# Quantised attention: one of two heads' scores read in one pass of 2048, the other in two of 1024

## The reference

```python
q = _fq_sym(q, axis=-1)      # 8 bit steps, one scale per row
k = _fq_sym(k, axis=-1)
v = _fq_sym(v, axis=2)
attn = jnp.einsum('bhqd,bhkd->bhqk', q, k)
attn = jax.nn.softmax(attn.astype(jnp.float32), axis=-1)
attn = _fq_unsigned(attn, axis=-1)     # round(x / (max/255)), 0..255
out = jnp.einsum('bhqk,bhkd->bhqd', attn, v)
return out @ Wp + bp
```

## Time and profile before

| what | us |
|---|---|
| median of 3 runs (2371.12 to 2379.82) | 2379.8 |
| the profiled execution, its own time | 2377.23 |
| its span | 2375.4 |
| busy in the span: PE / DVE / ACT / POOL | 2047.6 / 1697.0 / 1339.2 / 873.4 |
| busy share of the span: PE / DVE / ACT / POOL | 86% / 71% / 56% / 37% |
| the loop of the change, first to last instruction | 1384.4 to 2028.5 |

### The profile page before, as it was taken

The page is one execution under the profiler, slowest core; times in us unless marked ns, Lnnn a source line. Parts: engine busy times, 40 slices in busy tenths (PEclk is TensorE's granted clock), DMA queues, the critical chain, the costliest instruction groups (busy, mean ns, idle before and its releaser), DMA issues. The chain is left out here.

```text
span 2375.4 us, 49288 instructions
## 1 busy us (share of the span) xinstructions
PE 2047.6 (86%) x17593; PEld 1100.0 (46%) x17617; DVE 1697.0 (71%) x3048; ACT 1339.2 (56%) x1808; POOL 873.4 (37%) x730
## 2 busy tenths in 40 slices
PE   3776999999997785899996789999999999558855
PEld 1343555556564564488863423333333333434533
DVE  4775755555555557843356899999999999567975
ACT  3454633333335675633332568888888888445565
POOL 4750000000002561500053347777777777224301
PEclk8887999999997897999996755555555555788989
DMA  6343222222224007222322036666666665010110
GB/s 206 89 173 120 71 65 68 62 71 66 66 66 142 24 2 268 84 50 68 64 80 98 1 58 107 108 107 107 107 108 107 108 108 108 13 71 2 20 21 27
DMA packets 384870, 195.32 MB, mean 82 GB/s; under 512 B 312301, under 2 KB 355311, under 8 KB 382703
## 3 DMA queue, kind: packets, MB, share of 16 engines
q1 hardware_dynamic: 381617, 184.47, 32.5%
q0 software_dynamic: 3072, 8.39, 1.1%
HBM read 94.99 MB, written 23.09 MB: 50 GB/s over the span
## 5 line engine op out<-in xcount | busy, mean ns | idle before, releaser
L2429 POOL CAST qa_pT<-qa_eT 128x2048 bf16<-128x2048 uint8 x256 | 483.4, 1893 | 162.1 <-DMA qa_eT<-qa_e 120.8
L2442 PE MATMUL qa_S<-qa_kT,qa_qT 32*128 32x512 f16 x1024 | 514.4, 616 | 4.8 <-DVE qa_scores L2494 3.4
L2478 ACT ACTIVATE qa_e<-qa_scores,qa_nb 128x2048 uint8<-128x2048 f32 x256 | 510.4, 1994 | 4.4
L2494 DVE TENSOR_SCALAR_CACHE_REDUCE qa_scores<-qa_S,qa_sq,qa_mx 128x1024 f32<-128x1024 f32 x256 | 335.8, 1358 | 0.0
L2494 DVE TENSOR_SCALAR_CACHE_REDUCE qa_scores<-qa_S,qa_sq 128x1024 f32<-128x1024 f32 x256 | 320.2, 1297 | 3.4 <-PE qa_S L2442 3.4
L2452 PEld LDWEIGHTS qa_O<-qa_V,qa_pT 128*128 128x128 bf16 x4096 | 128.4, 105 | 215.6 <-issue 201.5
L1116 POOL MEMSET rms_nothing<- 128x512 f16 x1 | 0.5, 524 | 580.3 <-POOLq L3474 580.3
L973 PE MATMUL moe_G<-hT,moe_W 128*128 (+1 forms) x792 | 193.7, 381 | 7.1 <-DVE moe_zero L941 7.1
L982 PE MATMUL moe_O<-moe_W,moe_ap 128*128 (+1 forms) x1584 | 194.6, 273 | 4.3 <-DVE moe_ap L937 4.3
L913 ACT ACTIVATE moe_ap<-moe_a 128x512 f16<-128x512 f32 x132 | 83.1, 629 | 195.8 <-DVE moe_a L935 195.8
L973 PE MATMUL moe_U<-hT,moe_W 128*128 (+1 forms) x792 | 192.7, 379 | 0.0
(11 more groups left out here) (438 smaller groups left out, 3408.3 us busy)
## 6 DMA issues: line engine op xcount, KB each, us to landing
moe_wb<-weights_T SPq DMA_DIRECT2D x264, 128.0 KB, 2.9
moe_W<-in_moe_w SPq DMA_DIRECT2D x40, 384.0 KB, 11.9
moe_W<-in_moe_w SPq DMA_DIRECT2D x11, 1152.0 KB, 16.9
moe_xs_rows<-rms_nothing SPq DMA_DIRECT2D x46, 128.0 KB, 1.9
moe_ys_rows<-moe_ys SPq DMA_DIRECT2D x23, 256.0 KB, 2.1
conv_rows<-conv_parts SPq DMA_DIRECT2D x16, 256.0 KB, 2.9
qa_eT<-qa_e SPq DMA_TRANSPOSE x256, 3.1
conv_qst<-conv_rows SPq DMA_DIRECT2D x96, 32.0 KB
```

The source lines that it names most:

```text
L2429: nc.gpsimd.tensor_copy(pT[:, u % RING, :, :].rearrange("p (b r) q -> p b r q", r=2), pairs).then_inc(s_cast, 1)
L2442: last = nc.tensor.matmul(S[:, n % SLOTS, q * QW:(q + 1) * QW], qT[rows, g, t * P:(t + 1) * P], kT[rows, g, first:first + QW], start=True, ...
L2478: nc.scalar.activation(e8[:, u % RING, :], scores[:, u % RING, :], ACT.Exp, bias=nb[:, p % 2, i:i + 1], accum_out=sums[:, u:u + 1]).then_i ...
L2494: nc.vector.tensor_scalar(scores[:, u % RING, half * HW:(half + 1) * HW], S[:, n % SLOTS, :], sq[:, t, h:h + 1], mx[:, u % RING, 0:1] if h ...
```

## The change

PSUM is shared out anew: the scores have one ring of seven single banks in place of three slots of two, and the output has one bank in place of two. Of a pair k the unit 2k is read by DVE in one pass of 128 x 2048 (`whole`), the unit 2k+1 in two passes of 128 x 1024 (`first_half`, `second_half`), in the order first half, whole, second half. With k the banks change places: for even k the halves use banks 5, 6 and the whole 1 to 4, for odd k the halves use 0, 1 and the whole 2 to 5.

PE can fill a bank only once it has been read. So it fills three quarters of a whole pass ahead, and the fourth, like one quarter of the next first half, at the points that `passed(k, step)` names: it waits until DVE has finished pass number 3k + step. `values` of two units run in one go, once per pair. In `output`, ACT copies the single output bank ahead of the bias of a pair, where before it did so behind that pair's second exponential. DVE waits once per pair, before the first half, for both exponentials of the pair two back.

```diff
@@ sizes and the order of passes
-        SLOTS, HALVES, HW, QW = 3, 2, 1024, 512
-        mx = sb("mx", [P, RING, HALVES])
+        QW, BANKS = 512, 7
+        mx = sb("mx", [P, RING])
+        first_mx = sb("first_mx", [P, 2])
...
+        def first_half(k):
+            return 2 * k + 1, (0, 1), ((5, 6), (0, 1))[k % 2]
+
+        def whole(k):
+            return 2 * k, (0, 1, 2, 3), ((1, 2, 3, 4), (2, 3, 4, 5))[k % 2]
+
+        def second_half(k):
+            return 2 * k + 1, (2, 3), ((5, 6), (0, 1))[k % 2]
...
-            S = pctx.enter_context(nc.psum_tensor("qa_S", [P, SLOTS, HW], F32))
-            O = pctx.enter_context(nc.psum_tensor("qa_O", [P, 2, 512], F32))
+            S = pctx.enter_context(nc.psum_tensor("qa_S", [P, BANKS, QW], F32))
+            O = pctx.enter_context(nc.psum_tensor("qa_O", [P, NH * HD], F32))
@@ PE
+                    def quarters(a_pass, chosen):
+                        u, parts, banks = a_pass
                         t, h = divmod(u, NH)
                         g, j = divmod(h, GH)
                         rows = slice(j * SLOT, (j + 1) * SLOT)
+                        for i in chosen:
+                            last = nc.tensor.matmul(S[:, banks[i], :], qT[rows, g, t * P:(t + 1) * P], kT[rows, g, parts[i] * QW:(parts[i] + 1) * QW],
+                                                    start=True, stop=True)
+                        return last
...
-                        if h == 0 and t >= 2:
-                            pe.wait_ge(s_o, t - 1)
+                        if h == 0 and t >= 1:
+                            pe.wait_ge(s_o, t)
...
+                    def passed(k, step):
+                        if k >= 0:
+                            pe.wait_ge(s_mx, 3 * k + step + 1)
+
+                    def start_whole(k):
+                        quarters(whole(k), (1, 2, 3) if k % 2 == 0 else (0, 1, 2))
+
+                    quarters(first_half(0), (0, 1)).then_inc(s_S, 1)
+                    start_whole(0)
+                    for k in range(pairs_of_units):
+                        passed(k - 1, 2)
+                        quarters(whole(k), (0,) if k % 2 == 0 else (3,)).then_inc(s_S, 1)
+                        if k + 1 < pairs_of_units:
+                            quarters(first_half(k + 1), (1,) if k % 2 else (0,))
+                        passed(k, 0)
+                        quarters(second_half(k), (0, 1)).then_inc(s_S, 1)
+                        if 2 * k >= LAG:
+                            values(2 * k - LAG)
+                            values(2 * k + 1 - LAG)
+                        if k + 1 < pairs_of_units:
+                            passed(k, 1)
+                            quarters(first_half(k + 1), (0,) if k % 2 else (1,)).then_inc(s_S, 1)
+                            start_whole(k + 1)
+                    for u in range(units - LAG, units):
+                        values(u)
@@ ACT
                     for p in range(units // 2):
-                        act.wait_ge(s_mx, 4 * p + 4)
+                        if 2 * p % NH == LAG - 2 and 2 * p >= NH:
+                            output(2 * p // NH - 1)
+                        act.wait_ge(s_mx, 3 * p + 3)
...
-                            if u % NH == LAG - 1 and u >= NH:
-                                output(u // NH - 1)
@@ DVE
+                    def maximum(a_pass, n, so_far, greatest):
+                        u, parts, banks = a_pass
                         t, h = divmod(u, NH)
                         dve.wait_ge(s_S, n + 1)
...
+                        target = scores[:, u % RING, parts[0] * QW:(parts[-1] + 1) * QW].rearrange("p (b c) -> p b c", c=QW)
+                        nc.vector.tensor_scalar(target, S[:, banks[0]:banks[-1] + 1, :], sq[:, t, h:h + 1], so_far,
+                                                ALU.mult, ALU.max, accum_out=greatest).then_inc(s_mx, 1)
+
+                    for k in range(pairs_of_units):
+                        first, a, b = first_mx[:, k % 2:k % 2 + 1], 2 * k % RING, (2 * k + 1) % RING
+                        if 2 * k >= RING:
+                            dve.wait_ge(s_E, 2 * k + 2 - RING)
+                        maximum(first_half(k), 3 * k, None, first)
+                        maximum(whole(k), 3 * k + 1, None, mx[:, a:a + 1])
+                        dve.wait_ge(s_mx, 3 * k + 1)
+                        maximum(second_half(k), 3 * k + 2, first, mx[:, b:b + 1])
```

More of the change, by code:

```diff
@@ L2388, in quantised_attention @@
         units = NB * NH
+        pairs_of_units = units // 2
         RING = 4
         LAG = 8
[L2391 to L2392 removed]
+        QW, BANKS = 512, 7
+        mx = sb("mx", [P, RING])
+        first_mx = sb("first_mx", [P, 2])
         nb = sb("nb", [P, 2, 2])
@@ L2448, in values @@
                         pe.wait_ge(s_cast, u + 1)
-                        if h == 0 and t >= 2:
-                            pe.wait_ge(s_o, t - 1)
+                        if h == 0 and t >= 1:
+                            pe.wait_ge(s_o, t)
                         for b in range(NB):
-                            last = nc.tensor.matmul(O[:, t % 2, h * HD:(h + 1) * HD], pT[:, u % RING, b, :],
+                            last = nc.tensor.matmul(O[:, h * HD:(h + 1) * HD], pT[:, u % RING, b, :],
                                                     V[:, b, h * HD:(h + 1) * HD], start=b == 0, stop=b == NB - 1)
                         last.then_inc(s_V, 1)
[L2456 to L2462, removed]
+                    def passed(k, step):
[21 more added lines that the diff above has]
+                        values(u)
                 @block.scalar
@@ L2485, in _ @@
                 def _(dve):
-                    for n in range(2 * units):
-                        u, half = part(n)
+                    def maximum(a_pass, n, so_far, greatest):
+                        u, parts, banks = a_pass
                         t, h = divmod(u, NH)
                         dve.wait_ge(s_S, n + 1)
-                        if half:
-                            dve.wait_ge(s_mx, n - 1)
-                        elif u >= RING:
-                            dve.wait_ge(s_E, u - RING + 1)
-                        nc.vector.tensor_scalar(scores[:, u % RING, half * HW:(half + 1) * HW], S[:, n % SLOTS, :], sq[:, t, h:h + 1],
-                                                mx[:, u % RING, 0:1] if half else None, ALU.mult, ALU.max,
-                                                accum_out=mx[:, u % RING, half:half + 1]).then_inc(s_mx, 1)
+                        target = scores[:, u % RING, parts[0] * QW:(parts[-1] + 1) * QW].rearrange("p (b c) -> p b c", c=QW)
[9 more added lines that the diff above has]
+                        maximum(second_half(k), 3 * k + 2, first, mx[:, b:b + 1])
         scaled_projection(nc, sh, sums, wp, gate, NH)
```

16 lines of the change are left out of this document (2 added, 14 removed).

## The result

| | before | after |
|---|---|---|
| median, us | 2378.95 (4 runs, 2371.12 to 2379.82) | 2351.25 (4 runs, 2350.44 to 2356.99) |
| ratio, 95% interval | | 0.9896 [0.987, 0.9922] |
| profiled execution: own time, span | 2377.23, 2375.4 | 2351.08, 2348.4 |
| the loop, first score load to end of last output copy | 1384.4 to 2028.5: 644.1 | 1379.7 to 1999.8: 620.1 |

The time is 1% shorter, 27.7 us. Of the 27.0 us between the two spans the loop holds 24.0. The stages ahead of it, whose code is the same, took 4.7 us less, those behind it 1.7 us more.

The account below looks back on a forecast made before the run. The prediction took DVE, which never waits, to bound the loop at 4.94 us a pair. Saving 0.20 in each of 128 pairs gives 25.6 us, all else nothing: 2377.2 - 25.6 = 2351.6, forecast 2352, range 2343 to 2365.

Parts of the forecast that it names:

- What bounds: The loop before the change: DVE never waits and sets the pace, 4.94 us a pair.
- Part 1: DVE's passes: three a pair instead of four, 1.205 + 2.271 + 1.265 = 4.741 us, saving 0.20 a pair, 25.6 us.
- Part 2: PE's filling of score banks: each pass ready in time, tightest the whole pass with 0.38 us to spare; costs nothing.
- the mark: Time zero of the sum for PE's filling: DVE ends a whole pass and starts the second half.
- Part 3: ACT and the ring of scores: 0.29 us to spare, idle time shrinking from 0.62 to 0.42 a pair; costs nothing.
- the chain of 4.45: ACT's time from DVE's last pass of a pair to the second exponential's end: 4.45 us, within the pair's 4.74.
- Part 4: Values, casts, DMAs and the single output bank: all have room in the shorter pair; costs nothing.
- Part 5: The loop's ends: same first two products, and 10 us behind the last DVE pass as before; costs nothing.
- 1: Rival at PE's filling: row groups run in series, DVE waits 0.05 us a pair, 6 us in all, 2358; chance 0.06.
- 2: Rival at DVE's passes: the second scalar's 0.06 us belongs to the pair, so only 18 us go, 2359; chance 0.06.
- 3: Rival: the whole pass pays the fixed part again, or ACT's slack is used up; gain 7.7 us, 2369.5; chance 0.08.
- 4: Rival: PE becomes the bound at the whole pass, DVE waits 0.45 a pair, 32 us slower, 2409; chance 0.04.

Follow-up runs that it names:

- e11: Changed kernel with DVE multiplying by the constant 1.0 instead of the row's scale from SBUF (scale left out): loop 597.4 us, 2338.9 us in one run.
- e3: Changed kernel with the second half's pass without its second scalar: loop 612.3 us, median 2361.1, ratio to before 0.9881.
- e1: Changed kernel with the whole pass split into two passes of 1024, neither with a second scalar: loop 637.5 us, median 2390.4, ratio to before 0.9991.
- e2: Changed kernel with the whole pass split into two of 1024, the second with a second scalar: loop 645.5 us, median 2399.0, ratio to before 1.0031.
- e4: Changed kernel with heads reordered so four units in a row use the same rows of PE's array: loop 623.5 us, median 2371.0, ratio to before 0.9894.
- e10: Changed kernel with one quarter of the whole pass filled ahead in place of three: loop 674.1 us, median 2424.4, ratio to before 1.0125.
- e6: Changed kernel with ACT's copy of the output bank put back behind the second exponential: loop 647.0 us, median 2395.9, ratio to before 1.0022.
- e9: Changed kernel with a small exponential issued ahead of the loop, loading ACT's table early: loop 619.4 us, median 2372.3, ratio to before 0.9918.
- e12: Changed kernel with the row's scale moved from DVE to ACT's exponential and a bias per unit: loop 655.5 us, median 2403.9, ratio to before 1.0056.
- e8: Changed kernel with two small activations added on ACT before each pair's bias: loop 620.6 us, 2359.0 us in one run.

## Why the prediction was right

It gave 2352 (2343 to 2365); the median is 2351.25. The loop took 620.1 us where it had 618, and the whole time met it because the stages around the loop, whose code is the same, took 3 us less than in the profile before. Nothing in the prediction foresaw that: the agreement within 1 us is luck, that within 2 us in the loop is not. By its parts:

- **What bounds.** DVE, busy for the whole of each window before and after. e11 and e3 confirm it from the other side: whatever its passes lose, the loop loses, as far as 4.56 us a pair.
- **Part 1.** 1.205, 2.271 and 1.265 became 1.20, 2.27 and 1.27. The choice of 1.066 for the second 1024 columns, by the reduction of the earlier trace rows, held within 0.01; the tensor product's 1.04 would have been too low. The choice rested on a reduction that reads SBUF, so that its fit to a pass from PSUM was found by this run and not known before. The split into 0.14 of fixed part and 0.06 of second scalar is measured by e1 (0.136) and by e2 and e3 (0.0625 and 0.061); e11 adds that 0.06 of the 0.14 is the first scalar. The formula of the Trainium skill ("VectorE: DVE Perf Modes", section on the TRN2 errata) gives 0.125 for the fixed part. That is near the 0.136 of a pass with one scalar; it has no term for scalars, and the fixed part of a pass with none (0.07) and of one with two (1.27 - 1.07 = 0.20) lie on either side of it. The second scalar's share of the gain is 8 us.
- **Part 2.** DVE never waits for PE once the loop's first pass is filled. The whole pass is ready 0.45 early (predicted 0.38) because the fourth quarter did not stand behind the third: it started on its own release at 1704.42 and was ready 0.63 later, 2.02 after the second half's start where the sum had 2.09; the values end 4.58 after the mark (1707.61 - 1703.03; predicted 4.64). e4 and e10 show that this spare time was real and finite.
- **Part 3.** Right in the steady loop: ACT idles 0.43 a pair, as predicted 0.42. Wrong at the start: the chain of 4.45 was read in the middle of the loop and has a table load in its first pair, so that DVE waits 0.92 us there. That is the first miss.
- **Part 4.** Casts, DMAs and the single bank cost nothing in the loop, the bank only because the copy moved (e6).
- **Part 5.** "Nothing" was the second miss: the casts come three in a row at the end, and the stretch behind DVE's last row is 0.4 us longer. That the casts make it so is not shown: with three in a row it is 10.3 in e10 and 11.0 in e9, and of the kernel before there is one trace (10.2). Both misses together are 1.3 of 25.6 us.
- **Rivals.** 1: at full strength (e4) 3.4 us, and not present. 2: excluded by the 1.27 of the second half, by e2 and by e3. 3: a pass over three bank borders shows no second fixed part, 2.27 against 2.41. 4: its wait, and its price to 2 us, appear with only one quarter ahead (e10, loop 30 us above before), which the change avoids; its own cause, five products each with its load in series, did not show even in e4.

## What to carry to other kernels

Where one engine never waits, take its instructions by the distance of their starts and split each into a fixed part, a part per column and a part per operand; three rows of the trace gave this gain to 7%. Then compare every other engine's chain with the new, shorter period, and do so at the first and last round too, where a table load or a bunched queue stands that the steady loop doesn't show. Before moving work from the bounding engine to the next one, price it with that engine's own operands: here 0.18 us taken off DVE put 0.68 on ACT (4.99 of work a pair against 4.74 - 0.43 = 4.31), which had 0.43 idle.

## What the runs showed of the hardware

- A VectorE pass with a maximum, reading float32 from PSUM, costs start to start 0.07 us, 1.07 per 1024 columns, and 0.06 for each scalar read from SBUF: the multiplier at 1024 and at 2048 columns (e11, against a constant), the start of the maximum at 1024 (e2, e3, against none). A pass over four PSUM banks pays nothing at their borders: it takes 2.27, two passes over two banks each 2.41 (e1).
- A ScalarE activation pays 0.10 us for a scale from SBUF at 2048 columns, and lasts 0.37 with two operands from SBUF at one column, where the bias without them, of two columns, lasts 0.20 (e12). Small independent ones start 0.10 apart though each row lasts 0.20 (e8).
- Score products on 32 rows of the array overlap across row groups: the same six take 1.89 us with neighbouring heads in different groups and 2.31 with the heads of e4, where the five that the whole pass waits for share one group. All of it ran at a granted clock of 0.50, the lower level of 1.2 GHz, with PE busy for 99 to 100% of a window before the change, 82% after it, and 73% (e10) to 93% (e4) in the variants.
